# Three attentions of a two-layer decoder: each token group projected and added as soon as it is ready, and the next stage's first half begun inside the attention's last steps

## What is computed

```python
x = x + _L0_attn_ref(_layernorm(x), ...)        # gated delta rule, two chunks of 64, 2 heads of 128
x = x + _L0_xattn_ref(_layernorm(x), ctx, ctx)  # softmax attention on the context, 16 heads of 16
x = x + _L0_ffn_ref(_layernorm(x), ...)         # router, 4 experts of 512, best 2 mixed, layer norm
x = x + _L1_attn_ref(_layernorm(x), ...)        # causal self attention, one key/value head for all 16
x = x + _L1_xattn_ref(_layernorm(x), ctx, ctx)  # causal attention on the context
x = x + _L1_ffn_ref(_layernorm(x), ...)         # 8 experts of 128, GELU, best 2 summed
```

## Time and profile before

| | |
|---|---|
| median of 3 runs | 5361.09 us (5360.71 to 5361.69) |
| profiled execution: its own time | 5361.46 us |
| profiled execution: span from first to last instruction | 5359.7 us |
| mean granted TensorE clock | 0.961 |
| TensorE matmuls busy | 4697.3 us (88%) |
| VectorE / ScalarE / GpSimd busy | 77% / 44% / 74% |

### The profile page before, as it was taken

The page is one execution under the profiler, slowest core; times in us unless marked ns, Lnnn a source line. Parts: engine busy times, 40 slices in busy tenths (PEclk is TensorE's granted clock), DMA queues, the critical chain, the costliest instruction groups (busy, mean ns, idle before and its releaser), DMA issues.

```text
span 5359.7 us, 108430 instructions
## 1 busy us (share of the span) xinstructions
PE 4697.3 (88%) x28362; PEld 3072.0 (57%) x28362; DVE 4119.1 (77%) x11313; ACT 2322.5 (43%) x4480; POOL 3977.9 (74%) x12365
## 2 busy tenths in 40 slices
PE   1089999999999999999999999999999999899989
PEld 0065656656565565656556565665656556565655
DVE  8867777777777877787777777777777777777778
ACT  0044444454444444443454544445444444444444
POOL 6688585868858587785858868586895858678585
PEclk7599999999999999999999999999999999999999
DMA  3000000000000000000000000000000000000000
GB/s 90 12 9 9 21 1 25 5 9 21 9 21 1 25 5 9 21 1 29 1 13 17 9 21 1 25 5 9 21 9 21 1 25 6 9 21 6 17 1 17
DMA packets 61911, 78.34 MB, mean 15 GB/s; under 512 B 11168, under 2 KB 53808, under 8 KB 61232
## 3 DMA queue, kind: packets, MB, share of 16 engines
q1 hardware_dynamic: 52784, 62.42, 3.5%
q10 hardware_dynamic: 8448, 8.39, 0.5%
HBM read 45.04 MB, written 8.46 MB: 10 GB/s over the span
## 4 chain that ended last, share of the span: by engine, by line
PE 62%; DVE 22%; issue 8%; ACT 6%; SPq 1%; POOL 1%; DVEq 0%; DMA 0%; ACTq 0%; POOLq 0%
PE bank L1264 7%; PE bank L1297 5%; PE bank L1357 5%; PE bank L1183 5%; PE bank L1169 4%; PE bank L1383 3%; PE bank L1195 3%; PE bank L1217 3%; PE bank L1093 3%; DVE smax L1890 3%; PE bank L1100 3%; DVE arena L1500 2%; PE bank L1282 2%; ACT arena L856 2%; PE bank L1175 2%
## 5 line engine op out<-in xcount | busy, mean ns | idle before, releaser
L1890 DVE TENSOR_REDUCE smax<-bank 128x4 f32<-128x512 f32 x768 | 525.4, 684 | 82.8 <-PE bank L1175 37.7
L843 ACT ACTIVATE arena<-bank 128x512 f32<-128x512 f32 x768 | 455.1, 593 | 249.9 <-PE bank L1183 244.1
L1894 DVE TENSOR_TENSOR arena<-bank,smax 128x512 f32<-128x512 f32 x768 | 531.2, 692 | 26.5
L509 POOL TENSOR_TENSOR arena<-arena 128x1024 f32<-128x1024 f32 x17 | 32.2, 1893 | 664.8 <-DVE y_nat L1622 664.7
L1183 PE MATMUL bank<-ident,arena 128*128 128x128 f32 x3072 | 485.5, 281 | 42.3 <-ACT arena L830 25.0
L1264 PE MATMUL bank<-w,arena 128*128 128x512 f32 x1024 | 498.6, 619 | 14.0 <-DVE arena L1832 14.0
L1169 PE MATMUL bank<-arena 64*128 64x512 f32 x1536 | 441.1, 651 | 64.4 <-ACT arena L867 28.0
L1183 PEld LDWEIGHTS bank<-ident,arena 128*128 128x128 f32 x3072 | 346.6, 141 | 242.9 <-ACT arena L832 82.2
L1297 PE MATMUL bank<-w,arena 128*128 128x256 f32 x2048 | 454.1, 380 | 13.9 <-ACT arena L902 13.9
L830 ACT ACTIVATE arena<-arena,rstd 128x512 f32<-128x512 f32 x512 | 368.2, 719 | 199.9 <-DVE arena L1894 195.8
L648 POOL TENSOR_TENSOR acc_a<-acc_s,arena 128x32 f32<-128x32 f32 x1008 | 273.2, 271 | 225.9 <-DVE gate L2011 103.5
(11 more groups left out here) (437 smaller groups left out, 11925.4 us busy)
## 6 DMA issues: line engine op xcount, KB each, us to landing
arena<-in_x_dram SPq DMA_DIRECT2D x35, 512.0 KB, 3.6
xn_next<-arena SPq DMA_DIRECT2D x17, 512.0 KB, 2.9
arena<-cum_dram SPq DMA_DIRECT2D x17, 512.0 KB, 3.8
arena<-in_ctx_dram SPq DMA_DIRECT2D x16, 512.0 KB, 4.0
out_dram<-arena ACTq DMA_DIRECT2D x16, 512.0 KB, 3.2
xn<-xn_next SPq DMA_DIRECT2D x15, 512.0 KB, 2.9
w<-in_L_ffn_w_dram SPq DMA_DIRECT2D x8, 512.0 KB
w<-in_L_ffn_w_dram SPq DMA_DIRECT2D x1, 1024.0 KB
```

Source lines behind the costliest of these rows:

```text
L509: operation(*operands).then_inc(sum_step, 1)
L843: act.activation(PT[:, v % 2], bank[3 + v % 2][:, :].rearrange("p (h q) -> p h q", h=QH), ACT.Copy).then_inc(S["pt"], 1)
L1890: dve.tensor_reduce(smax[:, u, :], sc, AX, ALU.max).then_inc(S["s_max"], 1)
L1894: dve.tensor_tensor(Ssb[:, u % 4], sc, smax[:, u, :].unsqueeze(2).broadcast_to([P, QH, P]), ALU.subtract).then_inc(S["s_sub"], 1)
```

## The change

Projections. `project(a_no, g)` now stands at steps 11, 15, 19 and 23, as soon as group g has its `attT`. It writes to the upper half of bank 7. VectorE adds each group by itself (`add_group`), at steps 12, 16 and 20 and behind the loop, and takes its statistics there. Since bank 7 is shared, TensorE's transpose of group b + 1 (steps 13, 17, 21) now waits until group b has been added (`res`) and no longer for the copy of `attT`.

First halves. ScalarE takes the root of groups 0 and 1 at step 17, and VectorE refines it at step 18. TensorE transposes those two groups inside the tail (`half_features(s, 0, ...)`), the copies to `xT` are in two parts, and TensorE gets work of its own (`beside`): two of the `up(0, g)` in attention 0, the keys of attention 2 in attention 1. After attention 2 the gate logits and the first two hidden layers of the first two groups stand ahead of the second transposes. The 3 fillers of attention 0 become 4 in two places, and the 14 of attention 2 go.

Decays. Parts 0 to 5 of `decay_exponential` move to steps 5 to 10 of attention 2 (they were at 12 to 15 and 17), parts 6 and 7 to step 17, part 8 stays at step 21. GpSimd gets one more wait, for the transposes behind attention 0, ahead of an addition to `xres`.

```diff
@@ TensorE @@
+                def half_features(s, m, src, name, ready):
+                    if m:
+                        xT_ready(s, 0)
+                    pe.wait_ge(S[name], at(it, name, ready))
+                    for c in range(C):
+                        for g in (2 * m, 2 * m + 1):
+                            ins = tr(bank[XT_BANKS[s][c]][:, g * P:(g + 1) * P], src[:, g, c * P:(c + 1) * P], ident[:, :])
+                        ins.then_inc(S["xT_psum"], 1)
...
                             if b > 0:
-                                pe.wait_ge(S["attT"], at(it, "attT", a_no * G + b))
+                                pe.wait_ge(S["res"], at(it, "res", ADDED[a_no] + b))
...
-                        if u >= QUADS + 4 and u - QUADS - 4 < G - 1:
-                            project(a_no, u - QUADS - 4, w_out)
-
-                    project(a_no, G - 1, w_out)
+                        if u >= 8 and (u - 8) % 4 == 3 and (u - 8) // 4 < G:
+                            project(a_no, (u - 8) // 4, w_out)
+                        if u >= QUADS + 4:
+                            beside(u - QUADS - 4)
...
-                        ins = mm(bank[g // 2][:, (g % 2) * D:(g % 2 + 1) * D], attT[:, c, g * P:(g + 1) * P], w_out[:, c, :], start=(c == 0), stop=(c == C - 1))
-                    if g % 2:
-                        ins.then_inc(S["y_psum"], 1)
+                        ins = mm(bank[7][:, C * P:C * P + D], attT[:, c, g * P:(g + 1) * P], w_out[:, c, :], start=(c == 0), stop=(c == C - 1))
+                    ins.then_inc(S["y_psum"], 1)
@@ ScalarE, in attention @@
+                        if u == QUADS + 1:
+                            half_rstd(HALF_NORM[a_no], 0, 1)
+                        if (a_no, u) in ((0, QUADS + 5), (1, QUADS + 7), (2, QUADS + 6)):
+                            xT_copy((2, 4, 5)[a_no])
@@ VectorE, in attention @@
+                        if u >= 12 and u % 4 == 0:
+                            add_group(a_no, (u - 12) // 4)
+                        if u == QUADS + 2:
+                            half_root(HALF_NORM[a_no], 0)
+                            if a_no == 2:
+                                normed_rows(0)
+                        if (a_no, u) in ((0, QUADS + 4), (1, QUADS + 7), (2, QUADS + 6)):
+                            xT_copy((2, 4, 5)[a_no])
...
-                            if a_no == 2 and 12 <= u:
-                                decay_exponential(u - 12)
+                            if a_no == 2 and 5 <= u < 11:
+                                decay_exponential(u - 5)
...
+                def add_group(a_no, g):
+                    if a_no == 0 and g == 0:
+                        wait("bias_res", 1)
+                    wait("y_psum", 4 * a_no + g + 1)
+                    dve.tensor_tensor(xres[:, g, :], xres[:, g, :], bank[7][:, C * P:C * P + D], ALU.add).then_inc(S["res"], 1)
+                    wait("res", ADDED[a_no] + g + 1)
+                    dve.bn_stats(stats[:, g, :], xres[:, g, :]).then_inc(S["hl_stats"], 1)
+                    if g % 2:
+                        half_moments(HALF_NORM[a_no], g // 2)
@@ VectorE, behind attention 2 @@
-                layer_norm(5, xres, lambda m: add_y(2, 8, m))
-                xT_copy(5)
+                add_group(2, 3)
+                half_root(5, 1)
+                normed_rows(1)
+                xT_copy(5, 1)
```

More of the change, by code:

```diff
@@ L1319, in _, with third_keys @@
                 pe.wait_ge(S["q"], at(it, "q", 4))
-                attention(1, True, 1, Wcp)
-                for m in range(C):
+                def third_keys(m):
                     for c in range(C):
@@ L2023, in mixture_norm @@
                     ins.then_inc(S["res"], 1)
-                    wait("res", 4 + m + 1)
+                    wait("res", 6 + m + 1)
                 for e in range(E0 + 1):
                     if e < E0:
-                        for g in range(G):
-                            wait("up_psum", 4 * e + g + 1)
-                            dve.bn_stats(ust[:, g, :], bank[g][:, :]).then_inc(S["up_stats"], 1)
+                        for g in range(0 if e else 2, G):
+                            up_stats(e, g)
                         hidden_moments(e)
@@ L2085, in _ @@
                 attention(1)
-                for m in range(2):
-                    add_y(1, 6, m)
-                    half_stats(4, m, xres)
-                xT_copy(4)
+                add_group(1, 3)
                 for m in range(2):
```

156 lines of the change are left out of this document (98 added, 58 removed).

## The result

| | before | changed |
|---|---|---|
| median | 5360.9 us | 5468.94 us (5430.11 to 5471.92, 6 runs) |
| ratio, 95% interval | | 1.0184 [1.0165, 1.0204] |
| profiled execution: span, mean granted clock | 5359.7 us, 0.961 | 5440.3 us, 0.956 |

The change costs 1.84%, and I had forecast 0.5% to the good. (The ratio leaves out one run of the kernel before, 5819.93 us, and is not that of the medians, which are 108 us apart.) The changed kernel's runs fall into two groups (5430 and 5443; four of 5469 to 5472), and the profiled one took 5443.05 us. So the trace can explain 82 of the 108 us; what the longer runs add is not in it.

What follows compares the result with a forecast made beforehand. TensorE, busy for 88% of a pass, was taken as the bound, with gains only at three seams. -0.45 - 0.85 - 0.45 = -1.75 us a pass, 28 us in 16, gave 5361.1 - 28 = 5333 us; range 5302 to 5364.

Steps and rivals of the forecast that it cites:

- Seam 1: Attention 0 to the experts: idle time and fillers of 2.66 us become 2.2, -0.45 us a pass.
- Seam 2: Attention 1 to 2: shorter waits let the queries end 0.6 us earlier; -0.85 us a pass in all.
- The decays in attention 2: Parts 0 to 5 at steps 5 to 10: no wait for `au`, but a late division of group 0.
- No wait for `au`: Attention 2, decay part 0: GpSimd has `au` at 2108.6, VectorE needs it at 2108.7; nothing in hand.
- The wait at step 10: Attention 2: TensorE's second transposes wait 1.5 us for VectorE's division of group 0.
- VectorE took 1.34 us a step and parts 0 to 5 are small steps of 0.2: Attention 2: 21 small steps add 4.2 us in steps 5 to 10, making VectorE slower than TensorE.
- Seam 3: Behind attention 2: copy no earlier, hidden layers partly done ahead, some half clock; -0.45 us a pass.
- projection 1 ends near 2130: Attention 2: start of the times laid out for both engines, leading on to the last copy.
- the last copy 2143.4: Tail of attention 2: the last copy ends at 2143.4, before at 2143.37; no gain so far.
- VectorE's chain to `y_nat`: Behind the last copy: VectorE's unchanged 16.2 us to the decays lets TensorE win 1.6 us at most.
- The wait of 3 us for the GELU: Hidden layers behind attention 2: TensorE idle 3.2 us until ScalarE's first GELU, behind the gates' exponential.
- That of the slower side: Rival, chance 0.16: half clock in seam 3's tail without fillers, +1.4 us a pass, 5384 us.

Runs made afterwards that it cites:

- e8: Kernel before with the change in attention 1 and its seam alone: 5357.37 us, 0.9994.
- e17: Changed kernel with GpSimd's long subtraction made to start behind VectorE's subtraction of step 11: 5419.2 us, 1.0111.
- e11: Changed kernel with 11 fillers ahead of TensorE's wait at step 10 of attention 2: 5413.64 us, 1.0098.
- e1: Changed kernel with all parts of the decays at their old steps of attention 2: 5419.78 us, 1.0108.
- e5: e1 with 10 fillers behind attention 2, around the last projection and second transposes: 5403.51 us, 1.0081.
- e12: e5 with decay parts 6 to 8 behind the division of group 3, not ahead of it: 5363.0 us, 1.0005.
- e14: e13 with the gates ahead of the decays' quotient: 5399.94 us, 1.0074.
- e16: Kernel before with only the gates ahead of the decays' quotient: 5433.06 us, 1.0137.
- e13: e12 with no decay part ahead of any division (parts 4 to 8 moved): 5361.51 us, 1.0000.
- e3: Changed kernel with decay parts 4 and 5 one step later, at 10 and 11, behind group 0's division: 5416.76 us, 1.0105.

## Why the prediction was wrong

**Seam 1, -0.45: the waits went as laid out, the gain did not come.** To the end of `up` TensorE wins 0.21 us a pass, half of the sum. From the first maximum of attention 0 to the expert's transposes a pass takes 47.65 us before and 47.58 after: the wait of 2.23 us for VectorE behind the seam takes what TensorE has won. The step that failed is that I summed TensorE's idle time up to `up` and did not ask what it waits for next; to the router's gates it is even 0.27 us longer.

**Seam 2, -0.85: direction right, size 0.62**, and 0.60 in e8. The wait of 1.02 became 0.47, where I had said under 0.4.

**The decays in attention 2: here the sum failed, by 108 us with what followed.** No wait for `au`, as forecast. The wait at step 10, which I had forecast at 1.5 us, is 2.68. The step "VectorE took 1.34 us a step and parts 0 to 5 are small steps of 0.2" left out GpSimd: 0.79 of the 1.2 us difference is the one step that it holds up (e17 measures 0.66 less of wait). The steps were also too cheap in it: in e17, where GpSimd holds none of them up for more than 0.2 us, ten maxima and subtractions with 17 small steps between them take 17.35 us, which is 4.1 for the 17 steps and not 3.4. The larger fault is in the next sentence: "Everything of TensorE's attention is queued behind them" counted a wait as its own length. It also brought the clock down for the work behind it, and e11 shows that this was the greater part of what the decays cost inside attention 2, 1.90 of 3.44 us a pass: with the same late division and fillers in the gap, 55 of 108 us come back by the medians and 30 of 82 by the profiled runs. I had looked for half clock only behind attention 2, because there the kernel before had it.

**Seam 3, -0.45: wrong, in the steps "projection 1 ends near 2130" up to "the last copy 2143.4".** I put the last copy as far behind the first scores as before; from the first maximum it is 45.7 us and was 40.7. With the decays put back it is no better (45.8), so this is a fault of its own. I let VectorE do additions, statistics, roots and rows for half of the tokens and never checked the one division that is then late: that of group 3, behind parts 6 to 8, 1.83 us in e1 and e5 (0.60 in the changed kernel, where only part 8 stands there and TensorE is late already). In the kernel before the same parts stand at the same place and TensorE has no wait there (0.01 us in the mean); that the additions, statistics, roots and rows make the difference is my reading, not tested by itself. e12 measures the late division with all that follows from it: 40 us. The limit that I named behind the copy, VectorE's chain to `y_nat`, is there: e14 brings TensorE to it early and loses, and e16 makes the chain longer by a wait and loses that and more. But it is a limit and not what ends the stage before: TensorE came 1.8 us behind `y_nat` there and 1.5 in e13. It should have weighed more, for it leaves a shorter tail of TensorE's little to win unless VectorE's work shrinks too, and the change adds to that (busy 4184.1 us after, 4119.1 before). The wait of 3 us for the GELU is 1.67 in the sixth pass of the changed kernel, where slow halves of the hidden layers cover it, and 3.36 in e1.

**The rivals.** That of the slower side had the right mechanism, half clock, and the wrong place; its 5384 lacked the clock in attention 2. By 0.16 I gave it too little: two waits named as new (step 10 and the tail), each with TensorE idle for over a microsecond, were enough to doubt the clock at both.

**What stays open.** Why the same changed kernel takes 5430 to 5443 us in two runs and 5470 in four; why e3, e12 and e17 win a good part of their time at the start of the pass, far from what they changed; and how the 50 us of e17 divide over the causes.

## What to carry to other kernels

A wait of TensorE costs its length and can then cost the clock of what stands behind it: 11 fillers in a gap of 2.7 us were worth 55 us here, while a wait of 2.02 us brought the clock down in 12 passes of 16. When work is moved on VectorE, list each instruction that another engine waits for, in order, and what stands ahead of it now; nine small steps ahead of group 3's division cost 40 us, and the same steps behind it nothing. Read the wait again in each experiment, in all passes: e3 gave 52 us and had left its wait nearly as it was. And before summing what a seam gives to one engine, find the next wait behind it and the other engine that the stage needs: getting TensorE to `y_nat` earlier cost 38 us (e14), and one order of VectorE's work that made it wait for TensorE cost 71 (e16).

## What the runs showed of the hardware

A small VectorE instruction that reads SBUF can be held up until a GpSimd instruction ends. The step of 128x10 took 0.96 us in the changed kernel beside GpSimd's 128x1024 and ended 0.02 us behind it, and 0.97 us in e11, with the same 0.02. With GpSimd's instruction elsewhere it took 0.16. In the 18 traces together 104 small decay steps took over 0.4 us, and each ended 0.02 or 0.03 us behind a GpSimd instruction that was under way when it began. Most have two inputs in SBUF, but not all: the last step of part 3 (L1613 in e3, a `tensor_scalar` of one 128x10 tile with two constants) took up to 1.83 us. VectorE's reads of PSUM are not held up: in the kernel before the same GpSimd instruction ran from 2116.47 to 2118.36, and these two stood beside it at their usual 0.69 us.

```profile
2116.94 0.69 DVE L1890 TENSOR_REDUCE smax<-bank 128x4 f32<-128x512 f32 x1 [0.56 <-PE bank L1175]
2117.67 0.69 DVE L1894 TENSOR_TENSOR arena<-bank,smax 128x512 f32<-128x512 f32 x1
```

The Trainium skill ("SBUF — State Buffer", section "SBUF: two separate sides") says that VectorE and GpSimd share one pair of ports, that an instruction of VectorE with two SBUF inputs and a GpSimd instruction that reads SBUF exclude each other, and that the one that comes second stands still until the first is done. The traces agree: 1.89 us of GpSimd, and 0.79 us lost by an instruction that came 0.95 us into it. For the held-up step with one input this sentence gives no reason.
